# Moving the Q, K and V evictions from ScalarE to VectorE, and the attention scale from the Q eviction into the exponential

## The chip, the cores and the metric

The program runs on the eight cores of one Trainium2 chip. Every core executes the same program on its own two of the 16 sequences; nothing is exchanged between cores. The time of an execution is that of the slowest core, in microseconds (us).

## The reference

For x of shape (16, 2048, 1024), with one attention head of width 128 and a feed-forward part of width 4096:

```
xn  = layernorm(x)
Q, K, V = xn @ Wq, xn @ Wk, xn @ Wv
att = softmax(causal(Q @ K.T * 128**-0.5)) @ V @ Wo
h   = xn @ W1 + b1
h   = h + (cos(th)*wr + sin(th)*wi) * wi * sin(th + 0.1*h) * 0.1
out = x + att + relu(h) @ W2 + b2
```

## The kernel before

A core works through five stages, divided by barriers: stage 1 and attention for its first sequence, the same for its second, then one feed-forward stage over both. Each engine counts up the semaphore sbar at the end of a stage, and each waits for all of them before the next.

**Stage 1** (shown below) takes 16 tiles of 128 tokens. For each tile j:

- SP loads x into one of five buffers (L220). It waits with load j until ScalarE has centred tile j-5.
- VectorE computes mean and variance (two bn_stats, L313 and L314, and bn_aggr, L316).
- ScalarE takes the square root (L362) and writes the centred tile in bf16 (L367), one iteration behind VectorE.
- VectorE inverts the root (L323) and scales the identity matrix by it: diag_li (L328). It does this for tile j-2 after it has done the statistics of tile j. For the first sequence it also does some small operations on prep, a table of 32 columns, three per iteration up to j = 8.
- TensorE transposes the tile by eight products with diag_li (L440) into psTx. ScalarE copies psTx to xn_rg (L380), POOL stores that to the scratch tensor xn_scr (L236), which the feed-forward stage reads back.
- TensorE forms the tile's share of Q, K and V: 24 products, L412, L419 and L426, called qkv_slice(j) in the code. In TensorE's order it stands behind the transposes of tile j+1.

Four tiles make a group: psQ, psK and psVB are one bank each and hold 512 tokens. Only one copy of each exists, so between groups they have to be evicted to Q_fm, K_fm and V_tm. ScalarE does it (L385, L387, L388) right after the copy of the next group's first psTx, and this copy itself waits until the group's products are done, because xn_rg has room for four tiles. qkv_slice of the next group's first tile waits for the three evictions (semaphore sqke). The Q eviction multiplies by QSCALE. The fourth group's evictions stand behind the loop (L392 to L395).

For the first sequence ScalarE also computes an arctangent at j = 14 (L358), which needs another activation table before and after.

After its last store POOL issues the weight loads, W1 in the first sequence (L243) and W2 in the second (L250): four loads each, which convert f32 to bf16 and run while the attention stage runs. The attention blocks are opened with `nc.Block()` and not with no_gpsimd_drain, so that POOL ends them with a drain.

**Attention** takes 16 tiles of 128 queries, each with all keys up to the diagonal: products to psLogA and psLogB, a mask added by a product, exp on ScalarE with row sums (L641, L648, L657), the sums' inverse put on a diagonal by VectorE, transposes (L546), VectorE's evictions of them (L622), the products with V (L560) and ScalarE's copy to o_fm (L665).

**The feed-forward stage** runs 16 groups of 256 tokens through 32 slices of the hidden width; the output accumulates in psOut. It is the same in both kernels.

Of the kernel before, what the change touches and what calls it, by code (L numbers as in the profile page):

```python
# [11 lines left out]
AF = mybir.ActivationFunctionType  # L12
# [13 lines left out]
R1 = 512  # L26
NR1 = T // R1
R3 = 256
NR3 = T // R3
QSCALE = float(DK) ** -0.5  # L30
# [16 lines left out]
def build_nc():  # L47
# [23 lines left out]
    with ExitStack() as ctx:  # L71
# [20 lines left out]
        fc_sb = sbuf("fc_sb", [128, 8], F32)  # L92
# [5 lines left out]
        Q_fm = sbuf("Q_fm", [128, T], BF16)  # L98
# [30 lines left out]
        sqk = sem("sqk")  # L129
# [49 lines left out]
        try:  # L179
          for s in range(NSEQ):  # L180
# [3 lines left out]
            with ExitStack() as pctx:  # L184
# [120 lines left out]
                @blk.vector  # L305
                def _(v):
                    if bar_in:
                        v.wait_ge(sbar.h, bar_in)
                    for j in range(NT1 + 2):
                        if j < NT1:  # L310
                            p2 = 16 * (j % 4)
                            v.wait_ge(sxp[j % 5].h, sxp_b[j % 5] + 16 * (j // 5 + 1))
                            v.bn_stats(stats[:, p2 + 0:p2 + 6], x_sb[j % 5][:, 0:512])  # L313
                            v.bn_stats(stats[:, p2 + 6:p2 + 12], x_sb[j % 5][:, 512:1024])  # L314
                            v.drain()
                            ins = v.bn_aggr(stats[:, p2 + 12:p2 + 14],  # L316
                                            stats[:, p2 + 0:p2 + 12])
                            svar.inc(ins)
                        jj = j - 2
                        if jj >= 0:  # L320
                            p2 = 16 * (jj % 4)
                            v.wait_ge(srst.h, srst_b + jj + 1)
                            v.reciprocal(stats[:, p2 + 14:p2 + 15],  # L323
                                         stats[:, p2 + 15:p2 + 16])
                            if jj >= 2:
                                v.wait_ge(stx.h, stx_b + jj - 1)
                            v.drain()
                            ins = v.tensor_scalar(  # L328
                                diag_li[jj % 2][:], idn_sb[:],
                                stats[:, p2 + 14:p2 + 15], -1.0,  # L330
                                ALU.mult, ALU.mult)
                            sdg3.inc(ins)
                        if j < NT1:
                            for fn in pv.get(j, []):
                                fn(v)
                    v.drain()
                    v.sem_inc(sbar.h, 1)

                @blk.scalar
                def _(sc):  # L340
                    if bar_in:
                        sc.wait_ge(sbar.h, bar_in)
                    sc.wait_ge(sc0.h, 128)
                    if s == 0:
                        sc.activation(col(5), th_sb[:], AF.Sin, scale=1.0 / 16)
                        sc.activation(col(4), th_sb[:], AF.Sin, scale=1.0 / 32)
                        sc.drain()
                        sp1.inc(sc.activation(col(6), col(4), AF.Square), 2)
                    for j in range(NT1 + 2):
                        jj = j - 1  # L350
                        if s == 0 and j == 12:
                            sc.wait_ge(sp2.h, 1)
                            sc.drain()
                            sp3.inc(sc.sign(col(7), col(1)))
                        if s == 0 and j == 14:
                            sc.wait_ge(sp2.h, 2)
                            sc.drain()
                            sp3.inc(sc.activation(col(6), col(5), AF.Arctan))  # L358
                        if 0 <= jj < NT1:
                            p2 = 16 * (jj % 4)  # L360
                            sc.wait_ge(svar.h, svar_b + jj + 1)
                            srst.inc(sc.activation(stats[:, p2 + 15:p2 + 16],  # L362
                                                   stats[:, p2 + 13:p2 + 14],
                                                   AF.Sqrt, bias=fc_sb[:, 0:1]))
                            if jj >= 3:
                                sc.wait_ge(stx.h, stx_b + jj - 2)
                            ins = sc.activation(xn_tm[jj % 3], x_sb[jj % 5][:],  # L367
                                                AF.Identity, scale=-1.0,
                                                bias=stats[:, p2 + 12:p2 + 13])
                            sln.inc(ins)  # L370
                        je = j - 2
                        if 0 <= je < NT1:
                            r, tt = je // 4, je % 4
                            if tt == 0 and r > 0:
                                sc.wait_ge(sqk.h, sqk_b + 4 * r)
                            if je >= 4:
                                sc.wait_ge(sxnst[je % 4].h,
                                           sxnst_b[je % 4] + 16 * (je // 4))
                            sc.wait_ge(stx.h, stx_b + je + 1)
                            stxe.inc(sc.copy(xn_rg[:, tt * 1024:(tt + 1) * 1024],  # L380
                                             psTxB[je % 2][:]))
                            if tt == 0 and r >= 1:
                                rp = r - 1
                                sc.wait_ge(sqk.h, sqk_b + 4 * (rp + 1))
                                sqke.inc(sc.activation(Q_fm[:, rp * R1:(rp + 1) * R1],  # L385
                                                       psQ[:], AF.Copy, scale=QSCALE))
                                sqke.inc(sc.copy(K_fm[:, rp * R1:(rp + 1) * R1], psK[:]))  # L387
                                sqke.inc(sc.copy(V_tm[:, rp * R1:(rp + 1) * R1], psVB[:]))  # L388

                    rp = NR1 - 1  # L390
                    sc.wait_ge(sqk.h, sqk_b + 4 * (rp + 1))
                    sqke.inc(sc.activation(Q_fm[:, rp * R1:(rp + 1) * R1],  # L392
                                           psQ[:], AF.Copy, scale=QSCALE))
                    sqke.inc(sc.copy(K_fm[:, rp * R1:(rp + 1) * R1], psK[:]))
                    sqke.inc(sc.copy(V_tm[:, rp * R1:(rp + 1) * R1], psVB[:]))  # L395
                    sc.drain()
                    sc.sem_inc(sbar.h, 1)

# [57 lines left out]
            with ExitStack() as pctx:  # L456
# [172 lines left out]
                def _(sc):  # L629
                    sc.wait_ge(sbar.h, bar_in)  # L630
                    for qq in range(NT1 + 1):
                        j = qq - 1
                        if qq < NT1:
                            qi = qq
                            if qi >= 2:
                                sc.wait_ge(stx2.h, stx2_b + cum_sg[qi - 1])
                            sc.drain()
                            if qi >= 8:
                                sc.wait_ge(slgA.h, slgA_b + qi - 7)
                                a0 = 16 + 4 * (qi % 2)  # L640
                                ins = sc.activation(p2buf[qi % 2][:, 0:1024],  # L641
                                                    psLogA[:], AF.Exp,
                                                    bias=fc_sb[:, 1:2],
                                                    accum_out=stats[:, a0:a0 + 1])
                                se1.inc(ins)
                                sc.wait_ge(slg.h, slg_b + qi + 1)
                                sc.drain()
                                ins = sc.activation(  # L648
                                    p2buf[qi % 2][:, 1024:(qi + 1) * 128],
                                    psLogB[:, 0:(qi - 7) * 128], AF.Exp,  # L650
                                    bias=fc_sb[:, 1:2],
                                    accum_out=stats[:, a0 + 1:a0 + 2])
                                se1B.inc(ins)
                            else:
                                sc.wait_ge(slg.h, slg_b + qi + 1)
                                a0 = 16 + 4 * (qi % 2)
                                ins = sc.activation(p2buf[qi % 2][:, 0:(qi + 1) * 128],  # L657
                                                    psLogA[:, 0:(qi + 1) * 128],
                                                    AF.Exp, bias=fc_sb[:, 1:2],
                                                    accum_out=stats[:, a0:a0 + 1])  # L660
                                se1.inc(ins)
                        j2 = qq - 1
# [255 lines left out]
```

## Time and profile before

| | us |
|---|---|
| median of 3 runs | 1223.08 (1222.55 to 1224.01) |
| profiled execution, its time | 1225.54 |
| profiled execution, span of the slowest core (core 2) | 1223.8 |
| spans of the eight cores | 1209.9 to 1223.8 |
| core 2: stage 1, first sequence, until 78.7 | 78.7 |
| core 2: attention, first sequence, until 142.3 | 63.6 |
| core 2: stage 1, second sequence, until 194.3 | 52.0 |
| core 2: attention, second sequence, until the feed-forward stage's first product at 264.0 | 69.7 |
| core 2: feed-forward stage | 959.8 |

From 147.0 to 194.3 us, the second sequence's stage 1, ScalarE is busy for 39.3 of 47.3 us, TensorE for 35.8 and VectorE for 24.6. Of the whole span TensorE is busy for 89%.

A row of the timeline gives the start, the duration of one instruction or of a run of alike ones (x8), engine, line, operation, what is written and read, and in brackets how long the engine had been idle and what ended that. PEclk is the clock granted to TensorE as a share of 2.4 GHz.

### The profile page before, as it was taken

To read this page: it belongs to the slowest core of one execution; us is meant where nothing else is said; L and a number is where in the kernel's file an instruction comes from. 1 tells how busy PE (TensorE), PEld (TensorE's weight loads), DVE (VectorE), ACT (ScalarE), POOL (GpSimd) and SP (SyncE) were. 2 spreads that over 40 slices of the span, in tenths; PEclk is the share of its full clock that TensorE was granted. 3 is DMA by queue.
4 is the path that set the end of the run, shared out by engine and by line. 5 is a ranking of instruction groups with operands and counts; after the bars stand their busy time and mean duration, and the time that the engine had idled before them with its cause. 6 is when DMAs were issued, how large, how long until landed. Compare 5 with 4: busy or idle time off the path is not lost.

```text
span 1223.8 us, 23872 instructions; the slowest of 8 cores (1209.9 to 1223.8 us)
## 1 busy us (share of the span) xinstructions
PE 1085.5 (89%) x7936; PEld 736.5 (60%) x7936; DVE 453.2 (37%) x1007; ACT 596.0 (49%) x1285; POOL 37.0 (3%) x48
## 2 busy tenths in 40 slices
PE   0757676759999999999999999999999999999998
PEld 0745475546665666566656665666665666566665
DVE  2725662533333333333333333333333333333333
ACT  2865495525444545444545444545444544444444
POOL 1220031000000000000000000000000000000000
PEclk9976696789999999999999999999999999999999
DMA  7869687940202020202020202020202020202000
GB/s 159 245 118 195 143 251 126 168 119 1 87 1 87 1 87 1 87 1 86 2 87 2 87 1 87 2 86 2 87 1 87 1 87 1 87 1 87 22 32 36
DMA packets 47416, 87.13 MB, mean 71 GB/s; under 512 B 7106, under 2 KB 23490, under 8 KB 46274
## 3 DMA queue, kind: packets, MB, share of 16 engines
q1 hardware_dynamic: 36226, 59.39, 15.2%
q0 software_dynamic: 11072, 26.22, 11.9%
q8 instruction: 68, 1.11, 0.4%
q14 instruction: 50, 0.41, 0.1%
HBM read 78.25 MB, written 25.17 MB: 85 GB/s over the span
## 4 chain that ended last, share of the span: by engine, by line
PE 73%; DVEq 2%; DVE 2%; issue 1%; ACT 1%; ACTq 0%
PE psOut L847 37%; PE psW L821 36%; DVEq L767 2%; DVE probs L769 1%; ACT rb_sb L794 1%; DVE u_sb L746 1%; DVE out_sb L769 0%; PE psOut L837 0%; DVEq L774 0%; DVEq L745 0%; DVEq L766 0%; DVEq L743 0%; ACTq L793 0%; ACTq L791 0%; ACT ss_sb L786 0%
## 5 line engine op out<-in xcount | busy, mean ns | idle before, releaser
L821 PE MATMUL psW<-xn_r,W_sb 128*128 128x256 bf16 x4096 | 538.7, 275 | 8.5 <-PEq L456 8.5
L847 PE MATMUL psOut<-W_sb,rb_sb 128*128 128x512 bf16 x2048 | 531.6, 382 | 10.3 <-ACT rb_sb L794 10.3
L821 PEld LDWEIGHTS psW<-xn_r,W_sb 128*128 128x128 bf16 x4096 | 404.7, 99 | 169.2 <-issue 12.7
L746 DVE SCALAR_TENSOR_TENSOR u_sb<-ss_sb,Rp_sb,psW 128x256 f32<-128x256 bf16 x512 | 244.2, 480 | 592.0 <-ACT ss_sb L786 579.1
L786 ACT ACTIVATE ss_sb<-psW,phb_sb 128x256 bf16<-128x256 f32 x512 | 242.5, 474 | 444.1 <-PE psW L821 444.1
L847 PEld LDWEIGHTS psOut<-W_sb,rb_sb 128*128 128x128 bf16 x2048 | 200.6, 98 | 150.5 <-issue 19.2
L794 ACT ACTIVATE rb_sb<-u_sb,b_sb 128x256 bf16<-128x256 f32 x511 | 254.5, 498 | 57.1 <-DVE u_sb L746 55.1
L622 DVE CAST pT_big<-psT 128x512 bf16<-128x512 f32 (+2 forms) x80 | 48.9, 612 | 42.7 <-PE psT L546 38.5
L440 PE MATMUL psTx<-diag_li,probs 128*128 128x128 bf16 x176 | 15.9, 243 | 40.0 <-DVE diag_li L328 37.0
L546 PE MATMUL psT<-diag_li,xn_rg 128*128 128x128 bf16 x272 | 31.8, 263 | 17.8 <-DVE pT_big L622 15.6
L560 PE MATMUL psO<-pT_big,V_tm 128*128 128x128 bf16 x272 | 31.4, 259 | 17.0 <-DVE pT_big L622 16.3
L769 DVE TENSOR_TENSOR out_sb<-psOut,out_sb 128x512 f32<-128x512 f32 x32 | 20.6, 686 | 51.0 <-PE psOut L847 51.0
L380 ACT CAST xn_rg<-psTx 128x1024 bf16<-128x1024 f32 x32 | 32.4, 1014 | 12.5 <-PE psTx L440 7.6
L440 PEld LDWEIGHTS psTx<-diag_li,probs 128*128 128x128 bf16 x176 | 12.5, 109 | 41.5 <-issue 41.4
L546 PEld LDWEIGHTS psT<-diag_li,xn_rg 128*128 128x128 bf16 x272 | 22.4, 119 | 23.8 <-issue 23.7
L560 PEld LDWEIGHTS psO<-pT_big,V_tm 128*128 128x128 bf16 x272 | 20.2, 111 | 27.0 <-issue 25.4
L837 PE MATMUL psOut<-Wo_sb,o_fm 128*128 128x512 bf16 x64 | 23.6, 376 | 14.6 <-DVE probs L769 9.4
L665 ACT CAST o_fm<-psO 128x128 bf16<-128x128 f32 x32 | 8.5, 266 | 51.9 <-PE psO L560 51.9
L412 PE MATMUL psQ<-xn_rg,Wq_sb 128*128 128x128 bf16 x256 | 22.2, 236 | 11.2 <-ACT V_tm L388 10.9
L236 POOL DMA_DIRECT2D xn_scr<-xn_rg x32 | 27.1, 848 | 156.6 <-ACT xn_rg L380 156.6
L412 PEld LDWEIGHTS psQ<-xn_rg,Wq_sb 128*128 128x128 bf16 x256 | 17.6, 107 | 13.1 <-issue 12.8
L837 PEld LDWEIGHTS psOut<-Wo_sb,o_fm 128*128 128x128 bf16 x64 | 6.1, 96 | 31.2 <-issue 30.9
(91 smaller groups left out, 439.7 us busy)
## 6 DMA issues: line engine op xcount, KB each, us to landing
x_sb<-x SPq DMA_DIRECT2D x52, 512.0 KB, 5.6
W_sb<-w POOLq DMA_DIRECT2D x8, 2048.0 KB, 47.8
xn_scr<-xn_rg POOLq DMA_DIRECT2D x32, 256.0 KB, 4.3
xn_r<-xn_scr SPq DMA_DIRECT2D x16, 512.0 KB, 6.9
out<-out_sb SPq DMA_DIRECT2D x32, 256.0 KB, 2.1
out<-probs SPq DMA_DIRECT2D x32, 256.0 KB, 5.0
xn_r<-x SPq DMA_DIRECT2D x12, 512.0 KB, 6.3
Q_fm<-b2rep SPq DMA_DIRECT2D x1, 512.0 KB, 3.4
```

Of the source, the lines that this page charges most:

```text
L380: stxe.inc(sc.copy(xn_rg[:, tt * 1024:(tt + 1) * 1024], psTxB[je % 2][:]))
L412: t.matmul(psQ[:, tt * 128:(tt + 1) * 128], Wq_sb[:, ci * DK:(ci + 1) * DK], xn_rg[:, tt * 1024 + ci * 128: tt * 1024 + (ci + 1) * 128], s ...
L546: ins = t.matmul(psT2[b][:, (c % 4) * 128:(c % 4 + 1) * 128], p2buf[j % 2][:, c * 128:(c + 1) * 128], diag_li[j % 2][:], start=True, stop= ...
L560: ins = t.matmul(psO[j % 2][:], V_tm[:, c * DK:(c + 1) * DK], pT_big[c // 8][:, (c % 8) * 128:(c % 8 + 1) * 128], start=(c == 0), stop=(c ...
L622: (st2e if b == 0 else st2eV).inc(v.tensor_copy(pT_big[si // 2][:, (si % 2) * 512:(si % 2) * 512 + w], psT2[b][:, 0:w]))
L746: su2.inc(v.scalar_tensor_tensor(u2_sb[ci % 2][:], ss_sb[ci % 2][:], Rp_sb[:, c:c + 1], psW1[slot][:], ALU.mult, ALU.add))
L769: soadd.inc(v.tensor_tensor(out_sb2[j % 2][:, hh * 512:(hh + 1) * 512], psOut[tt][:, hh * 512:(hh + 1) * 512], out_sb2[j % 2][:, hh * 512: ...
L786: ssc3.inc(sc.activation(ss_sb[ci % 2][:], psW1[slot][:], AF.Sin, scale=0.1, bias=phb_sb[:, c:c + 1]))
L794: srb.inc(sc.activation(rb_sb[cp % 3][:], u2_sb[cp % 2][:], AF.Relu, bias=b1_sb[:, (cp % NCF):(cp % NCF) + 1]))
L821: ins = t.matmul(psW1[slot][:], W1_sb[:, k * DFF + c * 128: k * DFF + (c + 1) * 128], xn_r3[g % 2][:, k * R3:(k + 1) * R3], start=(k == 0) ...
L837: t.matmul(psOut[tt][:, h * 512:(h + 1) * 512], o_fm2[gg // NR3][:, c0:c0 + 128], Wo_sb[:, h * 512:(h + 1) * 512], start=True, stop=False, ...
L847: ins = t.matmul(psOut[tt][:, h * 512:(h + 1) * 512], rb_sb[cw % 3][:, tt * 128:(tt + 1) * 128], W2_sb[:, cc * D + h * 512: cc * D + (h + ...
```

## The change

VectorE does the evictions of Q, K and V. Those of group rp stand in its loop at j = 6, 10 and 14, behind the statistics of tile j, the diagonal of tile j-2 and the prep operations of that iteration, ahead of the statistics of tile j+1; those of the last group stand behind the loop. In front of each three it waits for the group's last product and drains. ScalarE's evictions are gone; its wait for the group's products, ahead of the next group's first copy to xn_rg, stays. Q is evicted without its factor, and the three exponentials get scale=QSCALE in its place.

```diff
@@ VectorE, stage 1, in the loop over j
+                        if j >= 6 and (j - 6) % 4 == 0:
+                            rp = (j - 6) // 4
+                            v.wait_ge(sqk.h, sqk_b + 4 * (rp + 1))
+                            v.drain()
+                            sqke.inc(v.tensor_copy(
+                                Q_fm[:, rp * R1:(rp + 1) * R1], psQ[:]))
+                            sqke.inc(v.tensor_copy(
+                                K_fm[:, rp * R1:(rp + 1) * R1], psK[:]))
+                            sqke.inc(v.tensor_copy(
+                                V_tm[:, rp * R1:(rp + 1) * R1], psVB[:]))
+                    rp = NR1 - 1
...
@@ ScalarE, stage 1, behind the copy to xn_rg
-                            if tt == 0 and r >= 1:
-                                rp = r - 1
-                                sc.wait_ge(sqk.h, sqk_b + 4 * (rp + 1))
-                                sqke.inc(sc.activation(Q_fm[:, rp * R1:(rp + 1) * R1],
-                                                       psQ[:], AF.Copy, scale=QSCALE))
-                                sqke.inc(sc.copy(K_fm[:, rp * R1:(rp + 1) * R1], psK[:]))
-                                sqke.inc(sc.copy(V_tm[:, rp * R1:(rp + 1) * R1], psVB[:]))
-
-                    rp = NR1 - 1
...
@@ ScalarE, attention, three times
                                                     psLogA[:], AF.Exp,
+                                                    scale=QSCALE,
                                                     bias=fc_sb[:, 1:2],
```

## Rows read from the trace of the kernel before

**Rows 1.** Stretches: engines' busy time, granted clock, DMA share, GB/s.
```profile
160.00:165.00 5.00, 4.15 (x68) 3.66 (x65) 4.27 (x12) 5.00 (x9) 1.50 (x2) 1.00 0.94 305
...
180.00:185.00 5.00, 2.52 (x32) 2.37 (x29) 0.42 (x2) 4.51 (x8) 0.84 (x1) 0.82 0.44 105
185.00:190.00 5.00, 5.00 (x77) 4.95 (x76) 0.42 (x2) 3.35 (x5) 1.69 (x2) 0.84 0.28 67
...
255.00:260.00 5.00, 0.38 (x4) 0.24 (x4) 0.00 (x0) 0.27 (x1) 0.00 (x0) 0.83 0.16 30
```

**Rows 2.** Timeline, core 2, around the second attention stage.
```profile
191.36 3.60 POOL L250 DMA_DIRECT2D W_sb<-w  x4
...
255.59 0.27 ACT L665 CAST o_fm<-psO 128x128 bf16<-128x128 f32 x1 [4.51 <-PE psO L560]
...
264.04 4.21 PE L821 MATMUL psW<-xn_r,W_sb 128*128 128x256 bf16 x19 [8.54 <-PEq L456]
```

**Rows 3.** Timeline, core 2, second sequence, from first to second group.
```profile
157.40 0.69 DVE L313 BATCH_NORM_STATS2 stats<-x_sb 128x6 f32<-128x512 f32 x1 [2.32 <-DMA x_sb<-x]
157.45 0.61 PE L426 MATMUL psVB<-Wv_sb,xn_rg 128*128 128x128 bf16 x8
...
158.01 0.68 DVE L314 BATCH_NORM_STATS2 stats<-x_sb 128x6 f32<-128x512 f32 x1
158.26 1.01 ACT L380 CAST xn_rg<-psTx 128x1024 bf16<-128x1024 f32 x1 [0.65 <-PE psVB L426]
...
159.11 0.25 DVE L328 TENSOR_SCALAR diag_li<-idn_sb,stats 128x128 bf16<-128x128 bf16 x1
159.17 0.60 ACT L385 ACTIVATE Q_fm<-psQ 128x512 bf16<-128x512 f32 x1
159.27 0.69 DVE L313 BATCH_NORM_STATS2 stats<-xn_r 128x6 f32<-128x512 f32 x1
...
159.61 0.61 PE L440 MATMUL psTx<-diag_li,pT_big 128*128 128x128 bf16 x8 [1.55 <-DVE diag_li L328]
...
160.99 0.61 PE L412 MATMUL psQ<-xn_rg,Wq_sb 128*128 128x128 bf16 x8 [0.77 <-ACT V_tm L388]
...
161.84 1.03 ACT L380 CAST xn_rg<-psTx 128x1024 bf16<-128x1024 f32 x1
```

**Rows 4.** Timeline, core 2, last products of further groups, both sequences.
```profile
39.73 0.61 PE L426 MATMUL psVB<-Wv_sb,xn_rg 128*128 128x128 bf16 x8
...
51.14 0.61 PE L426 MATMUL psVB<-Wv_sb,xn_rg 128*128 128x128 bf16 x8
...
62.16 0.61 PE L426 MATMUL psVB<-Wv_sb,xn_rg 128*128 128x128 bf16 x8
...
168.26 0.61 PE L426 MATMUL psVB<-Wv_sb,xn_rg 128*128 128x128 bf16 x8
...
179.68 0.61 PE L426 MATMUL psVB<-Wv_sb,xn_rg 128*128 128x128 bf16 x8
```

**Rows 5.** Timeline, core 2: the pace of VectorE and of ScalarE.
```profile
33.50 0.69 DVE L313 BATCH_NORM_STATS2 stats<-x_sb 128x6 f32<-128x512 f32 x1
...
36.19 0.69 DVE L313 BATCH_NORM_STATS2 stats<-x_sb 128x6 f32<-128x512 f32 x1
...
163.97 1.03 ACT L380 CAST xn_rg<-psTx 128x1024 bf16<-128x1024 f32 x1
```

**Rows 6.** Groups by shape, until 280 us: VectorE's casts of 512 columns.
```profile
L622 DVE CAST pT_big<-psT 128x512 bf16<-128x512 f32 x56 | 38.7, 692 | 36.6 <-PE psT L546 33.9 <-issue 0.2
```

**Rows 7.** Timeline, core 2: TensorE's first product behind two evictions.
```profile
54.77 0.61 PE L412 MATMUL psQ<-xn_rg,Wq_sb 128*128 128x128 bf16 x8 [2.50 <-ACT V_tm L388]
...
183.22 1.01 PE L412 MATMUL psQ<-xn_rg,Wq_sb 128*128 128x128 bf16 x8 [2.48 <-ACT V_tm L388]
```

**Rows 8.** Timeline, core 2: ScalarE around the first sequence's last group.
```profile
65.26 0.99 ACT L380 CAST xn_rg<-psTx 128x1024 bf16<-128x1024 f32 x1
...
68.83 1.02 ACT L380 CAST xn_rg<-psTx 128x1024 bf16<-128x1024 f32 x1
```

More of the change, by code:

```diff
@@ L335, in _ @@
                                 fn(v)
+                        if j >= 6 and (j - 6) % 4 == 0:
[9 more added lines that the diff above has]
+                    rp = NR1 - 1
+                    v.wait_ge(sqk.h, sqk_b + 4 * (rp + 1))
+                    v.drain()
+                    sqke.inc(v.tensor_copy(
+                        Q_fm[:, rp * R1:(rp + 1) * R1], psQ[:]))
+                    sqke.inc(v.tensor_copy(
+                        K_fm[:, rp * R1:(rp + 1) * R1], psK[:]))
+                    sqke.inc(v.tensor_copy(
+                        V_tm[:, rp * R1:(rp + 1) * R1], psVB[:]))
                     v.drain()
@@ L381, in _ @@
                                              psTxB[je % 2][:]))
-                            if tt == 0 and r >= 1:
-                                rp = r - 1
-                                sc.wait_ge(sqk.h, sqk_b + 4 * (rp + 1))
-                                sqke.inc(sc.activation(Q_fm[:, rp * R1:(rp + 1) * R1],
-                                                       psQ[:], AF.Copy, scale=QSCALE))
-                                sqke.inc(sc.copy(K_fm[:, rp * R1:(rp + 1) * R1], psK[:]))
-                                sqke.inc(sc.copy(V_tm[:, rp * R1:(rp + 1) * R1], psVB[:]))
-                    rp = NR1 - 1
[L391 to L395, printed above, removed]
                     sc.drain()
@@ L650, in _ @@
                                     psLogB[:, 0:(qi - 7) * 128], AF.Exp,
+                                    scale=QSCALE,
                                     bias=fc_sb[:, 1:2],
@@ L658, in _ @@
                                                     psLogA[:, 0:(qi + 1) * 128],
-                                                    AF.Exp, bias=fc_sb[:, 1:2],
+                                                    AF.Exp, scale=QSCALE,
+                                                    bias=fc_sb[:, 1:2],
                                                     accum_out=stats[:, a0:a0 + 1])
```

## The prediction

> **What bounds the kernel now.** I read the spans of all cores first, then the page's slices, then the busy time by stage, then the timeline of stage 1 and of the way into the feed-forward stage. The feed-forward stage holds 959.8 us of core 2's span of 1223.8 and is not touched, so the change can only move its start, 264.04 us [rows 2]. What sets that start is not the second attention stage's arithmetic: ScalarE's last copy of it ends at 255.86, the next product comes at 264.04, and in between only DMA runs, at a share of 0.16 [rows 1, 2]. That is the tail of the W2 loads, which POOL issued at 191.36, behind the last store of stage 1, and which its drain waits for. So on this core the end follows stage 1's last copies; whatever delays them by a microsecond delays W2 and the end by one.
>
> In stage 1 one place matters: the passage from one group of four tiles to the next. Let T be the end of a group's last product, 157.45 + 0.61 = 158.06 in the second sequence [rows 3]. ScalarE copies the next tile at T+0.20, then evicts Q, K and V. The diagonal of the tile after (number 5) leaves VectorE at 159.11, TensorE transposes at T+1.55, then waits until 160.99 for the evictions. ScalarE's copy of this tile starts at 161.84, T+3.78, and the following copy 2.13 later (163.97) [rows 3, 5]. Inside the group ScalarE sets the pace with 2.13 per tile; VectorE needs 159.27 - 157.40 = 1.87 per tile [rows 3]. The intervals from T to T are 11.41 and 11.02 in the first sequence, 10.81 and 11.42 in the second [rows 3, 4].
>
> **The change, part by part.**
>
> ScalarE loses three evictions at each passage. They held it from 159.17, and TensorE resumed on the third at 160.99 [rows 3]. That is about 1.4 us of ScalarE time, worth something only if the diagonal of tile 5 is there early. It is not any more, as the next part shows.
>
> VectorE gets the wait and the three copies ahead of the statistics of tile 7, and the diagonal of tile 5 stands behind these statistics. So what is queued behind the waiting VectorE is: two bn_stats and a bn_aggr (for which ScalarE's root of tile 7 waits, and behind it SP's load of tile 12), and the diagonal of tile 5, for which TensorE waits, and after it ScalarE and POOL's store. A cast of 512 columns out of PSUM takes 0.69 [rows 6]; two VectorE instructions in a row start 158.01 - 157.40 = 0.61 apart [rows 3]. I take release and drain as the 0.20 that ScalarE needs now [rows 3], so the third cast lets go at T + 0.20 + 3 x 0.61 + about 0.1 = T+2.1 (T+2.3 if none overlap). From the first bn_stats to the diagonal are 159.11 - 157.40 = 1.71, from there to TensorE's transposes 0.50, and 0.7 on to ScalarE's copy (0.61 and a release of 0.1) [rows 3]. So the transposes of tile 5 start at T + 2.1 + 1.71 + 0.50 = T+4.3 and its copy at T+5.0, where it is T+3.78 now: **1.2 us later at a passage**. TensorE is idle for some 4 us there. Everything cheap that used to cover the diagonal has gone: it was made while the products of the old group still ran.
>
> Then the rest of the group. ScalarE: copy 7 starts at 5.0 + 2 x 2.13 = T+9.3, ends at 10.3, and the last products take 0.1 + 1.5 (three runs of eight, 0.45 apart, the last of 0.61): T+12.0. VectorE: from T+2.1 three tiles of 1.87 and then 1.71 to the diagonal of tile 8, 0.5 to TensorE, 0.45 to the products and 1.5 for them: T+11.9. Both give an interval of 12.0. Against the measured ones [rows 3, 4]:
> - second sequence, first and second interval: 12.0 - 10.81 = +1.2 and 12.0 - 11.42 = +0.6;
> - first sequence, second interval: 12.0 - 11.02 = +1.0;
> - first sequence, first interval: VectorE has the prep operations too and takes 36.19 - 33.50 = 2.69 per tile [rows 5] for tiles 7 and 8, some 2.1 for tile 9. Tile 8's diagonal is then at 2.1 + 2 x 2.69 + 2.1 + 1.71 = T+11.3, the last product ends at T+13.7: 13.7 - 11.41 = +2.3.
>
> The last group. In the second sequence its end hangs on TensorE: three times transposes and products of one tile at 1.78 (four runs of eight, 0.45 apart), then 1.5, from T+4.3: T+11.1 at full clock. Now the last evictions wait for a product that ends 11.03 after T (ScalarE's idle time ends at 191.41): +0.1. In the first sequence ScalarE is late at this passage because of the arctangent and its tables: T is 62.77, and its copy 12 starts only at 65.26, copy 13 at 68.83 [rows 4, 8]. With the evictions gone copy 13 can follow copy 12 by 2.13, once VectorE's diagonal has come: T+5.0 = 67.8. This is 1.0 earlier, of which TensorE's tail keeps about 0.4: -0.4.
>
> The evictions behind the loop are on VectorE 2.1 us from T, on ScalarE 0.1 + about 1.7: +0.3, counted once, for the first sequence alone. In the second the W2 loads end later than attention by far more than this [rows 2].
>
> The exponentials get a factor. The nearest row is the Q eviction, which carries the same factor and takes 0.60 [rows 3]; 48 exponentials cost nothing by it, and 0.5 us if each costs 0.01. I take 0.
>
> Sum without the clock: 2.3 + 1.0 - 0.4 + 0.3 + 1.2 + 0.6 + 0.1 = +5.1.
>
> **The clock.** TensorE now sits idle for some 4 us at each of the six passages. Today's idle stretches there are at most 2.5 us long, and their outcome differs: behind 2.48 us the products run at 1.2 GHz (eight in 1.01), behind 2.50 at 2.4 GHz (eight in 0.61) [rows 7]. One such slow stretch shows as 0.82 and 0.84 of the clock in two slices of 5 us: (0.18 + 0.16) x 5 / 0.5 = 3.4 us at half speed, 1.7 us of lost work [rows 1]. Where TensorE has slack little of that reaches the end; my chains have about 0.5 to 0.9 of slack in the middle groups, so up to 1.2 reaches T there (three intervals, 3.6), 1.7 in the second sequence's last group, and almost nothing in the first interval, which waits for VectorE. If all fell: +5.3. I take half, +2.7. The Trainium skill's page "TensorE: Matmul & The Clock Gate", section "HAM oscillation — how this bites in real kernels", says that a stream of matmuls broken by long idle gaps falls back to the lower clock at every gap; by it the sum would be +10.4 and not +7.8. The rows above show both outcomes behind gaps of 2.5 us, and none of 4 us inside stage 1.
>
> **Sum:** +7.8, on the profiled execution 1225.5 to 1233.3. It stands 2.5 above the median, so the median goes to **1231**.
>
> **The rivals.**
> - *The clock falls at every passage, and costs more in the group than I allow.* +5.1 + 5.3 = +10.4, with VectorE's casts at no overlap (6 x 0.2) +11.6, and to +15 if the delays add up behind each other in the chains: 1235 to 1238. For it: the longer idle time. Against: one of the two present ones of 2.5 us did not trip it.
> - *DMA hides it.* From 160 to 165 us the DMA share is 0.94 at 305 GB/s, and VectorE waits 2.32 us for the x of tile 7 at 157.40 [rows 1, 3]. A group moves four loads of 512 KB and four stores of 256 KB, 3.1 MB, about 10.3 us at this rate. If stage 1 ran by DMA, VectorE would only wait for Q, K, V where it waits for x today, and nothing would be lost: 0 to +2, 1223 to 1225. Against: my interval of 12.0 is longer than 10.3, and the wait for x at 157.40 ended before ScalarE needed that diagonal.
> - *ScalarE's relief wins.* If ScalarE is the late one at a passage, taking 1.43 us off it brings the copy of tile 5 forward. This happens where its copy 4 starts later than T+1.4, as at the first sequence's arctangent (T+2.5). At all six passages it would be -8.6: 1214.5. For it: ScalarE is the busiest engine of stage 1 and sets the pace inside a group. Against: elsewhere copy 4 starts at T+0.20 [rows 3], long before that point.
> - *The W2 tail changes its length.* The 7.6 us between attention's end and the feed-forward stage are a DMA tail at a share of 0.16 [rows 1, 2]. Moved against other traffic it could be shorter or longer by some 2 us; it widens the range in both directions.
>
> **How the numbers follow.** My forecast (+4 to +10) has 0.62, the dearer clock 0.16, DMA cover 0.13, ScalarE's relief 0.09. 0.2% is 2.4 us, about what a measurement of this kernel tells from no change. Slower 0.78, same 0.13, faster 0.09. The range reaches from 1225 (upper end of the DMA case) to 1238 (upper end of the clock case).
>
> **What would show it.** VectorE has 24 more casts of 512 columns from psQ, psK and psVB, of 0.69 each. TensorE's idle time before L440 ends on VectorE's diagonal at six passages, after about 4 us, and its wait for the evictions is gone. The intervals from T to T are about 12 to 13.5 us. ScalarE's idle time before its copies to xn_rg grows. The granted clock in stage 1 is lower. POOL issues W2 some 5 to 10 us later than 191.36; the feed-forward stage is as long as before. I am wrong if VectorE's copies end well before T+2, if the intervals stay under 11.5, or if the feed-forward stage starts at a time that does not follow W2's issue.

## The result, and the profile after

| | before | changed |
|---|---|---|
| median of 8 runs each, us | 1224.21 | 1236.55 |
| ratio | | 1.0102 (1.009 to 1.0114) |
| profiled execution, its time | 1225.54 | 1235.43 |
| its span, slowest core | 1223.8 | 1233.5 |

The kernel became slower by 1.02%, 12.5 us (11.0 to 14.0); forecast were +7.8. Each median includes one execution of over 1300 us, which the ratio leaves out.

T is again the end of a group's last product. The passage from the second to the third group of the second sequence, changed kernel, core 2, from the timeline:

```profile
172.91 0.61 PE L431 MATMUL psVB<-Wv_sb,xn_rg 128*128 128x128 bf16 x8
173.68 0.69 DVE L340 CAST Q_fm<-psQ 128x512 bf16<-128x512 f32 x1 [3.71 <-PE psVB L431]
173.72 1.01 ACT L399 CAST xn_rg<-psTx 128x1024 bf16<-128x1024 f32 x1 [0.99 <-PE psVB L431]
174.28 0.68 DVE L342 CAST K_fm<-psK 128x512 bf16<-128x512 f32 x1
...
174.88 0.68 DVE L344 CAST V_tm<-psVB 128x512 bf16<-128x512 f32 x1
...
175.48 0.68 DVE L313 BATCH_NORM_STATS2 stats<-x_sb 128x6 f32<-128x512 f32 x1
...
177.17 0.25 DVE L328 TENSOR_SCALAR diag_li<-idn_sb,stats 128x128 bf16<-128x128 bf16 x1
...
177.68 1.01 PE L445 MATMUL psTx<-diag_li,probs 128*128 128x128 bf16 x8 [4.16 <-DVE diag_li L328]
...
178.78 1.01 ACT L399 CAST xn_rg<-psTx 128x1024 bf16<-128x1024 f32 x1 [2.82 <-PE psTx L445]
...
180.19 1.06 PE L431 MATMUL psVB<-Wv_sb,xn_rg 128*128 128x128 bf16 x8
...
182.74 0.61 PE L424 MATMUL psK<-xn_rg,Wk_sb 128*128 128x128 bf16 x8
...
186.76 0.61 PE L431 MATMUL psVB<-Wv_sb,xn_rg 128*128 128x128 bf16 x8
```

Beside [rows 3]: T is 173.52. VectorE sits idle for 3.71 us until 173.68, casts Q, K and V, and only then does the statistics; the diagonal comes at T+3.65, TensorE transposes at T+4.16 (it was T+1.55), ScalarE's second copy starts at T+5.26 (it was T+3.78). ScalarE, relieved of 1.43 us, spends 2.82 us idle in their place. From 177.68 to 182.7 eight products take 1.01 to 1.06 us, at 182.74 again 0.61: TensorE's clock. The third group ends at 187.37, an interval of 13.85.

The stretches of the changed kernel, core 2 (engines' busy time, granted clock, DMA share, GB/s), 5 us from the end of the idle time, and the second stage 1 as a whole:

```profile
177.50:182.50 5.00, 4.83 (x46) 4.86 (x47) 4.63 (x13) 2.55 (x4) 0.85 (x1) 0.50 0.57 163
149.20:203.90 54.70, 38.24 (x513) 37.38 (x514) 30.75 (x81) 33.58 (x45) 16.59 (x20) 0.78 0.65 184
```

and the same stage of the kernel before:

```profile
147.30:194.50 47.20, 35.80 (x513) 33.96 (x514) 24.34 (x69) 38.98 (x57) 16.63 (x20) 0.86 0.72 214
```

The granted clock is 0.50, 1.2 GHz, over a stretch in which TensorE is busy for 4.83 of 5.00 us, right behind 4.16 us of idle time. Over the stage it falls from 0.86 to 0.78. The passage one group earlier on the same core had the same idle time and another outcome at first:

```profile
164.58 0.61 PE L445 MATMUL psTx<-diag_li,pT_big 128*128 128x128 bf16 x8 [4.16 <-DVE diag_li L328]
...
166.16 1.06 PE L431 MATMUL psVB<-Wv_sb,xn_rg 128*128 128x128 bf16 x8
...
169.33 0.61 PE L431 MATMUL psVB<-Wv_sb,xn_rg 128*128 128x128 bf16 x8
```

Here the products start at 0.61 and become slow about 1.1 us later, until about 169.1, some 3.4 us of slow time; this interval is 13.09. Each of this core's six passages has such a stretch. So have those of the other seven cores: in the timelines of one profiled execution each, all 48 passages of the changed kernel show TensorE idle for 4.16 us and behind it a stretch of at least 2.5 us in which eight products take over 0.85 us. In the kernel before 24 of 48 show one, though TensorE's single waits there are shorter. Between the first and the last T of each sequence such slow time adds up to 25.2 us per core in the changed kernel and to 11.5 in the kernel before.

TensorE's waits from 20 to 205 us, core 2, changed kernel (in total, times, longest; the longest is the program's start), and then before:

```profile
PE psTx L445 <- DVE diag_li L328: 59.4, 13, 24.9
```

```profile
PE psTx L440 <- DVE diag_li L328: 39.6, 8, 27.1
PE psQ L412 <- ACT V_tm L388: 10.9, 6, 2.5
```

The wait for the evictions has gone and that for the diagonal has grown by more: without the start 34.5 us, before 12.5 + 10.9 = 23.4.

The evictions themselves, as groups by shape, and the exit of the second stage 1, changed kernel, core 2:

```profile
L340 DVE CAST Q_fm<-psQ 128x512 bf16<-128x512 f32 x6 | 4.1, 691 | 17.0 <-PE psVB L431 17.0
L344 DVE CAST V_tm<-psVB 128x512 bf16<-128x512 f32 x6 | 4.1, 679 | 0.0
```

```profile
200.13 0.61 PE L431 MATMUL psVB<-Wv_sb,xn_rg 128*128 128x128 bf16 x8
200.78 3.60 POOL L250 DMA_DIRECT2D W_sb<-w  x4
...
202.11 0.68 DVE L353 CAST V_tm<-psVB 128x512 bf16<-128x512 f32 x1
203.74 2.17 SPq L583 DMA_DIRECT2D xn_r<-xn_scr  x2
```

A cast takes 0.68 to 0.69, as [rows 6]. POOL issues W2 at 200.78, 9.4 later than in [rows 2].

To compare the kernels I took the ends of the groups' last products from the timelines of all eight cores of one profiled execution each. A "first" interval runs from the first group's T to the second's, and so on. The mean intervals, in us; "sum" is that of the six, and "measured" is (ratio - 1) x 1224:

| kernel | first sequence | second sequence | sum | against before | measured |
|---|---|---|---|---|---|
| before | 11.2, 11.2, 13.6 | 10.7, 11.0, 10.5 | 68.1 | | |
| changed | 13.8, 13.2, 12.9 | 13.4, 13.8, 13.4 | 80.4 | +12.2 | +12.5 |
| e1_fill | 13.8, 12.4, 11.1 | 11.8, 11.8, 11.1 | 71.9 | +3.8 | +3.8 |
| e2_later | 12.6, 10.5, 13.2 | 10.4, 11.0, 8.9 | 66.5 | -1.6 | -0.7 |
| e4_wait | 12.7, 11.4, 13.8 | 11.4, 11.0, 10.9 | 71.2 | +3.1 | +2.2 |
| e7_best | 12.5, 10.5, 12.0 | 10.7, 10.8, 8.8 | 65.3 | -2.9 | -2.1 |
| e8_fill_before | 10.7, 11.3, 12.4 | 10.7, 10.9, 9.9 | 66.0 | -2.1 | -2.1 |

The six intervals account for the whole difference within about 1 us in every row. That is also their own scatter: e3_scale, which does the same work in stage 1 as the kernel before, has a sum of 69.1 against 68.1. The delay is made in stage 1 and passes through everything behind it.

### The profile page after: what moved, and what is told of

It reads as the page before. It is cut to its first block, busy times and chain, and to the rows that moved or that the text cites. A ratio compares the mean times of both kernels' runs of the same rounds, so it can differ in the third digit from the quotient of the medians.

```text
span 1233.5 us, 23880 instructions; the slowest of 8 cores (1227.8 to 1233.5 us)
## 1 busy us (share of the span) xinstructions
PE 1089.8 (88%) x7936; PEld 741.8 (60%) x7936; DVE 466.9 (38%) x1031; ACT 584.7 (47%) x1261; POOL 37.0 (3%) x48
## 4 chain that ended last, share of the span: by engine, by line
PE 72%; DVEq 2%; DVE 2%; issue 1%; ACT 1%; ACTq 0%
PE psOut L855 36%; PE psW L829 36%; DVEq L775 2%; DVE probs L777 1%; ACT rb_sb L802 1%; DVE u_sb L754 0%; DVE out_sb L777 0%; PE psOut L845 0%; DVEq L782 0%; DVEq L753 0%; DVEq L774 0%; DVEq L751 0%; ACTq L801 0%; ACTq L799 0%; ACT ss_sb L794 0%
## 5 line engine op out<-in xcount | busy, mean ns | idle before, releaser
L445 PEld LDWEIGHTS psTx<-diag_li,probs 128*128 128x128 bf16 x176 | 13.6, 115 | 56.9 <-issue 56.9
L424 PE MATMUL psK<-xn_rg,Wk_sb 128*128 128x128 bf16 x256 | 23.2, 243 | 0.0
```

The source lines that it names most:

```text
L445: ins = t.matmul(psTxB[j % 2][:, c * 128:(c + 1) * 128], xn_tm[j % 3][:, c * 128:(c + 1) * 128], diag_li[j % 2][:], start=True, stop=True, ...
```

## The experiments

**e1_fill: keep TensorE's clock.** The changed kernel plus:

```diff
                         if j >= 1:
                             qkv_slice(j - 1)
+                        if j in (4, 8, 12):
+                            for _ in range(16):
+                                t.matmul(psD[:], idn_sb[:], Wq_sb[:, 0:512],
+                                         start=True, stop=True,
+                                         skip_group_check=True)
```

> The changed kernel, with 16 extra products of 512 columns that TensorE writes to the free eighth PSUM bank behind the last product of the first three groups of each sequence (96 in all; their result is not read). They fill about 3.5 us of the 4.2 us in which TensorE waits for VectorE's diagonal. Theory (order of VectorE's work costs 1.2 us at a passage, and the clock that falls in the idle time costs 1 to 2 us more): the granted clock in both stages 1 goes back to 0.95 or more, the intervals between group ends fall from 13.1 to 13.9 to about 12.0 (12.7 to 13.8 stay in the first sequence's first interval, which waits for VectorE), and the time falls by 6 to 9 us against the changed kernel, to 1227 to 1231. Rival (the intervals are long because of VectorE's own work or of DMA, the clock only fell along with it): intervals and time stay within 2 us of the changed kernel, 1235 to 1238.

Measured: 1226.65 us, ratio 1.0031 (1.0018 to 1.0043). Core 2, timeline, and the two stages 1:

```profile
172.37 0.61 PE L432 MATMUL psVB<-Wv_sb,xn_rg 128*128 128x128 bf16 x8
173.03 3.40 PE L456 MATMUL psD<-Wq_sb,idn_sb 128*128 128x512 bf16 x15
...
176.63 0.26 DVE L329 TENSOR_SCALAR diag_li<-idn_sb,stats 128x128 bf16<-128x128 bf16 x1
...
177.14 0.61 PE L446 MATMUL psTx<-diag_li,probs 128*128 128x128 bf16 x8 [0.70 <-DVE diag_li L329]
...
177.83 1.01 ACT L400 CAST xn_rg<-psTx 128x1024 bf16<-128x1024 f32 x1 [2.41 <-PE psTx L446]
...
184.14 0.61 PE L432 MATMUL psVB<-Wv_sb,xn_rg 128*128 128x128 bf16 x8
```

```profile
27.00:81.00 54.00, 43.08 (x559) 35.40 (x562) 36.56 (x108) 36.08 (x48) 16.40 (x20) 1.00 0.70 186
149.80:199.00 49.20, 42.94 (x558) 35.82 (x562) 30.58 (x81) 33.12 (x45) 16.59 (x20) 0.93 0.76 205
```

The diagonal is exactly as late as in the changed kernel (T+3.65, transposes at T+4.16 from T = 172.98), but the products behind it take 0.61, and the interval is 11.78 in place of 13.85. The granted clock of the second stage 1 is 0.93, under the 0.95 expected; the missing part lies in its first group, ahead of any passage, and from the first T on it is 1.00. Slow time between the sequences' first and last T is 0.2 us per core, where it was 25.2. Work whose result nobody reads, put into idle time, makes the changed kernel 0.7% faster. So of the 12.5 us, 8.7 are the lower clock behind the late diagonal, and 3.8 are left. The 3.8 are not the late diagonal alone, because the kernel before loses some time to its clock as well: e8_fill_before, below, makes it 5.9 with the clock kept in both.

**e2_later: the same casts one iteration later.**

```diff
-                        if j >= 6 and (j - 6) % 4 == 0:
-                            rp = (j - 6) // 4
+                        if j in (7, 11, 15):
+                            rp = (j - 7) // 4
```

> The changed kernel with VectorE's evictions in the loop one iteration later, at j = 7, 11 and 15, so that the diagonal of the next group's second tile is made before VectorE waits. Theory (the place in VectorE's order is what costs): TensorE transposes that tile at about T+1.5 as in the kernel before, the copy follows at T+2.4 instead of T+3.8, intervals of 9.7 to 10.9 us, where DMA (3.1 MB a group) begins to set the pace; clock as before; the time is 0 to 6 us below the kernel before, 1218 to 1224. Rival (VectorE is too busy for these casts wherever they stand): intervals of 12 us or more and over 1230.

Measured: 1222.81 us, ratio 0.9994 (0.9984 to 1.0004). Core 2, timeline, and one stretch:

```profile
157.13 0.61 PE L431 MATMUL psVB<-Wv_sb,xn_rg 128*128 128x128 bf16 x8
157.13 0.25 DVE L328 TENSOR_SCALAR diag_li<-idn_sb,stats 128x128 bf16<-128x128 bf16 x1
157.63 0.61 PE L445 MATMUL psTx<-diag_li,pT_big 128*128 128x128 bf16 x8
...
159.10 0.68 DVE L344 CAST V_tm<-psVB 128x512 bf16<-128x512 f32 x1
...
160.04 0.61 PE L417 MATMUL psQ<-xn_rg,Wq_sb 128*128 128x128 bf16 x8 [1.79 <-DVE V_tm L344]
160.09 1.00 ACT L399 CAST xn_rg<-psTx 128x1024 bf16<-128x1024 f32 x1
```

```profile
165.00:170.00 5.00, 3.64 (x60) 3.17 (x57) 4.03 (x12) 3.53 (x6) 0.84 (x1) 1.00 1.04 321
```

The diagonal leaves VectorE while the old group's last products still run; ScalarE's second copy starts at 160.09, T+2.35 from T = 157.74, where it was T+3.78 in [rows 3]. So ScalarE's relief is worth its 1.43 us here. VectorE has as many casts as in the changed kernel: the place in its order, with the clock that falls behind it, cost 13 us (1.0102 against 0.9994), not the work. The time is that of the kernel before, but not every interval is: the first sequence's first, in which VectorE also has the prep operations, is 1.4 us longer, and the second sequence's last is 1.6 shorter (8.9 against 10.5). The first two intervals of the second sequence hardly fall below those of before. The DMA share is 1.04 there, and VectorE waits 5.4 us in that stage for x on core 2 (before 5.8, with the changed kernel 0.6); I read this as DMA setting the pace, but no run made the loads lighter. At the passage of the first sequence's last group all eight cores still have a slow stretch.

**e3_scale: the factor alone.** The evictions stay on ScalarE, Q as a plain copy, `scale=QSCALE` in the three exponentials.

> The kernel before, evictions on ScalarE, with only the factor moved: Q is evicted by a plain copy and the three exponentials get scale=QSCALE. Theory: no change, within 1 us of the kernel before. Rival (a factor in an exponential costs 10 ns or more each): 0.5 to 1 us slower, with the ACTIVATE rows of the exponentials longer by that.

Measured: 1224.1 us, ratio 0.9998 (0.9979 to 1.0018). A group by shape of e3_scale, core 2; before, the same instructions (L648) took 1114 on the mean:

```profile
L647 ACT ACTIVATE xn_rg<-psLogB,fc_sb 128x1024 bf16<-128x1024 f32 x2 | 2.2, 1113 | 0.2
```

The 16 exponentials of full width from psLogA take 1113 with the factor and 1114 without. The rows show no cost of the factor; the time alone, with an interval of 0.2% to either side, could not have told 0.5 us from nothing.

**e4_wait: the wait without the casts.** The kernel before plus, at the same place in VectorE's loop:

```diff
+                        if j >= 6 and (j - 6) % 4 == 0:
+                            rp = (j - 6) // 4
+                            v.wait_ge(sqk.h, sqk_b + 4 * (rp + 1))
+                            v.drain()
```

> The kernel before with only VectorE's wait for the group's last product and its drain, at j = 6, 10 and 14; the evictions stay on ScalarE. Theory (the casts ahead of the statistics are what makes the diagonal late, the wait by itself is covered by ScalarE's evictions): the diagonal of the next group's second tile leaves VectorE at about T+2.0, TensorE transposes at T+2.5, ScalarE's copy stays at about T+3.8; time within 2 us of before. Rival (the wait alone costs): intervals 1 us longer or more and 5 us or more in all.

Measured: 1225.5 us, ratio 1.0018 (1.0008 to 1.0029): slower by 2.2 us, a little beyond what the theory expected. Core 0, timeline:

```profile
160.13 0.61 PE L430 MATMUL psVB<-Wv_sb,xn_rg 128*128 128x128 bf16 x8
...
162.67 0.69 DVE L328 TENSOR_SCALAR diag_li<-idn_sb,stats 128x128 bf16<-128x128 bf16 x1
...
163.61 0.61 PE L444 MATMUL psTx<-diag_li,pT_big 128*128 128x128 bf16 x8 [2.87 <-DVE diag_li L328]
...
164.52 1.03 ACT L384 CAST xn_rg<-psTx 128x1024 bf16<-128x1024 f32 x1
...
166.76 0.69 DVE L313 BATCH_NORM_STATS2 stats<-xn_r 128x6 f32<-128x512 f32 x1 [1.98 <-DMA xn_r<-x]
```

From T = 160.74 ScalarE's second copy starts at T+3.78, to the hundredth as before: at the passage the wait is covered. What it costs shows in the first intervals of both sequences (+1.4 and +0.7 in the table). In the first sequence VectorE has the prep operations to do; the two cores whose clock holds there (1 and 5) take 13.0. In the second sequence it is mostly the clock again, because one wait of 2.87 us has taken the place of 1.55 and 0.77:

```profile
176.44 1.01 PE L444 MATMUL psTx<-diag_li,probs 128*128 128x128 bf16 x8 [2.87 <-DVE diag_li L328]
```

This is the same core one passage later, and here the products behind 2.87 us run at half speed. Of the second sequence's first intervals those of cores 1, 3, 6 and 7 have a stretch like this and take 11.3 to 11.7 us; those of cores 2, 4 and 5 have none of this length and take 10.7 to 10.8, as before. Core 0 takes 12.8: it comes to wait for x (1.98 us) a tile further on; whether VectorE's wait caused that was not tried. Of all 48 passages of e4_wait 30 have a slow stretch.

**e5_w2_before and e6_w2_after: without the last W2 load,** before and changed, `range(4)` to `range(3)` and the counts of swr lowered by 16. These two kernels leave out the fourth quarter of W2: the feed-forward stage reads the third in its place (`cc % 24`), with as many products as before and a wrong output.

> The kernel before without the last of the four W2 loads (4 MB of 16 MB read less; the feed-forward stage takes the third quarter of W2 twice in its place, with as many products as before). Theory (the tail of the W2 loads sets the feed-forward stage's start on the slow cores): the gap from ScalarE's last copy of the second attention stage to the first feed-forward product, 1.1 to 8.2 us on the eight cores, is 1 to 2 us on all of them, and the slowest core ends 4 to 8 us earlier, 1215 to 1220. Rival (the gap is the drain itself and does not hang on the loads): gap and time stay, 1223 to 1225.

> The changed kernel with the same cut in the W2 loads. Theory (the delay of stage 1 goes through to the end whichever of the two, arithmetic or W2, ends last): the distance to the kernel before with the same cut stays 10 to 14 us, so 1226 to 1233. Rival (the W2 tail swallowed part of the delay, or made part of it): the distance is under 8 us or over 16 us.

Measured: 1217.69 us, 0.9953 (0.9935 to 0.9971), and 1230.64 us, 1.0058 (1.0042 to 1.0073). The feed-forward stage's first products with the idle time before them, e5_w2_before, core 7:

```profile
L821 PE MATMUL psW<-xn_r,W_sb x152: 272/273/421, 256.9 to 289.7; 128*128 128x256 bf16 x152
its engine sat idle before it (us, times) until:
  issue: 1.7, 1
  PEq L456: 1.5, 1
```

The gap from ScalarE's last attention copy to the first product is 1.1 to 1.2 us on all eight cores of both kernels; it was 1.1 to 8.2 before ([rows 2]) and 1.1 to 8.6 with the change. So the tail of the W2 loads is what the late cores wait for, and it costs the kernel 5.8 us (3.5 to 8.0). The quotient of the two ratios is 1.0058 / 0.9953 = 1.0105, that of the two kernels with all of W2 1.0102: the tail neither swallows nor makes a part of the delay.

**e8_fill_before: the clock in the kernel before.** Six products of 512 columns where TensorE waits for the evictions, ahead of `qkv_slice(j - 1)` at j = 5, 9 and 13.

> The kernel before with 6 extra products of 512 columns (1.3 us) between the transposes of a group's second tile and the products of its first, where TensorE waits for ScalarE's evictions (at j = 5, 9, 13). Theory (with idle time of at most 2.5 us the clock falls only at some passages, and there it costs 0.4 to 0.7 us each): clock in both stages 1 at 0.97 or more, time 0 to 3 us below the kernel before. Rival (a low clock costs the kernel before as much as the changed one, so it explains no part of the difference): 6 us faster or more.

Measured: 1221.25 us, ratio 0.9983 (0.9971 to 0.9994), 2.1 us faster. The granted clock of core 2's two stages 1 is 0.96 and 0.94, less than the 0.97 expected, but slow time between the sequences' first and last T falls from 11.5 to 1.3 us per core, and one passage of 48 keeps a stretch. The lower clock costs the kernel before about a quarter of what it costs the changed one. With the clock kept in both, the two kernels are 1.0031 / 0.9983 = 1.0048 apart, 5.9 us.

**e7_best: e2_later with both ideas.** Seven such products at j = 4, 8 and 12, and K of the last group on ScalarE:

```diff
+                    sc.wait_ge(sqk.h, sqk_b + 4 * NR1)
+                    sqke.inc(sc.copy(K_fm[:, (NR1 - 1) * R1:NR1 * R1], psK[:]))
                     sc.drain()
```

> The version with VectorE's evictions one iteration later, with two additions: 7 extra products of 512 columns in TensorE's idle time behind the first three groups, and in the last group K evicted by ScalarE beside Q and V on VectorE. Theory (DMA now sets the pace inside the second sequence's stage 1, the clock costs little): 0 to 3 us faster than without the additions, so 1219 to 1223, mostly from the first sequence. Rival (the clock still costs in that version): 5 us faster or more.

Measured: 1221.64 us, ratio 0.9983 (0.997 to 0.9995). It beats the kernel before by 2.1 us, no more than the filling alone does in e8_fill_before. Against e2_later the gain is in the first sequence (its intervals add up to 35.0, there 36.2), none in the second (30.2, there 30.3).

**e9_w2_late: e7_best, and the feed-forward stage no longer waits for all of W2.**

```diff
-                            swr.inc(g.dma_start(dstw, srcw), 16)
+                            (swl if jw == 3 else swr).inc(
+                                g.dma_start(dstw, srcw), 16)
...
-                blk = pctx.enter_context(nc.Block())
+                blk = pctx.enter_context(nc.Block(no_gpsimd_drain=(s == 1)))
...
                             t.wait_ge(srb.h, srb_b + cw + 1)
+                            if cw == 24:
+                                t.wait_ge(swl.h, 16)
```

> The version with VectorE's evictions one iteration later, the extra products and K on ScalarE behind the loop, and with the feed-forward stage no longer waiting for all of W2: the fourth load has a semaphore of its own, for which TensorE waits at the 25th slice of the first group, some 40 us into that stage, and the second attention stage ends without POOL's drain. Theory (on the slow cores the tail of the W2 loads sets the feed-forward stage's start): the gap from ScalarE's last copy to the first feed-forward product is 1 to 3 us on all cores where it was 1.1 to 10.1, and the time is 3 to 7 us below the same version without this, 1214 to 1219. Rival (the first three loads end as late as the fourth, because they share the DMA engines): gap and time as without it, 1221 to 1223.

Measured: 1216.64 us, ratio 0.9938 (0.9915 to 0.9961), the fastest version. The gap is 1.1 to 1.2 us on all cores, where it was 1.1 to 10.1 in e7_best. About 5.5 of its 7.6 us come from the wait that the prediction met on its way to the end (0.9938 against e7_best's 0.9983), and the other 2.1 are e7_best's. The semaphore of its own and the missing drain were not tried apart.

## Why the prediction was right, and where its sizes were off

The direction, the place and the mechanism were right: VectorE's diagonal comes late, TensorE's idle time and the chain behind it grow, and the clock falls. The size was not: 12.5 us lie outside the band of +4 to +10 to which I gave 0.62, and inside that of the rival with the dearer clock.

- *The passage, 1.2 us.* Right: transposes at T+4.16 for a forecast T+4.3; the copy at T+4.85 with the clock kept (177.83 in e1_fill), T+5.26 without, for T+5.0. e2_later shows that it is the order: the same casts behind the diagonal cost nothing on balance.
- *The intervals, 12.0 and 13.7 in the first.* With the clock kept they are 11.8, 12.4 and 13.8. For the second sequence's last group I had 11.1, and e1_fill has 11.1.
- *The sum without the clock, +5.1.* Measured +3.8 (2.2 to 5.3). The largest difference is the first sequence's last interval, -2.5 where I had -0.4. The 13.6 of before contain a stretch at 1.2 GHz on all eight cores, which I had left in my figure for after; e8_fill_before puts about 1.1 on it (12.4). The remaining 1.3 (12.4 to 11.1) I read as ScalarE's relief at the arctangent, of which I had let only 0.4 arrive: on core 2 its copy 13 starts at T+4.9 in e1_fill and at T+5.6 in e8_fill_before. Against e8_fill_before, where both keep their clock, the intervals differ by 71.9 - 66.0 = 5.9.
- *The exit, +0.3.* Not there. From the first stage 1's last T to attention's first product are 3.2 us on the mean before and 3.2 after. VectorE's casts end later than ScalarE's did, but in the second stage 1 the next stage starts 203.74 - 202.79 = 0.95 us behind the last one, where behind ScalarE's it took 1.37 (192.97 to 194.34).
- *The exponentials, 0.* Right, by the rows of e3_scale.
- *The clock, +2.7.* This is the term that was mis-sized: it is 12.5 - 3.8 = 8.7 us. It went wrong in two steps. First, I took half of the passages, and all 48 have a stretch. Half was the share of the kernel before (24 of 48), whose waits are shorter; I carried it over to waits of 4.16 us. I also wrote that the present waits are at most 2.5 us long, and core 2 has one of 2.95, with a slow stretch two microseconds on:

```profile
65.71 0.61 PE L440 MATMUL psTx<-diag_li,probs 128*128 128x128 bf16 x8 [2.95 <-ACT probs L367]
...
67.97 1.01 PE L412 MATMUL psQ<-xn_rg,Wq_sb 128*128 128x128 bf16 x8 [1.65 <-ACT V_tm L388]
```

  Second, the price if all fell was +5.3, and it is 80.4 - 71.9 = 8.5 by the intervals. The stretch is 3.4 to 5.2 us long on core 2, where I had 3.4 from [rows 1]. By interval, e1_fill against the changed kernel: 0 in the first, which waits for VectorE, as I had it; +0.8, +1.6 and +2.0 where I allowed 1.2 each; +2.3 for 1.7 in the second sequence's last group; and +1.8 in the first sequence's last group, for which I had no clock term at all, without a reason. The rival of a dearer clock was the case that came true; I gave it 1235 to 1238 and 0.16. The rule of the Trainium skill's page "TensorE: Matmul & The Clock Gate", section "HAM oscillation — how this bites in real kernels", that the clock falls at every long gap, agrees with this trace, at 0.50 behind 4.16 us of idle time, and would have been the better choice than one half.
- *DMA hides it.* Not with intervals of over 12 us, as forecast: VectorE's waits for x before L313 in core 2's second stage 1 fall from 5.8 us to 0.6. What keeps e2_later from its gain in the second sequence is probably DMA; that was not shown.
- *W2 sets the end.* Right as a mechanism, by e5_w2_before; and the delay passes through in full, by e6_w2_after.

## What to carry to other kernels

Work moved to an engine with room costs by what stands behind it in that engine's order: three casts and a wait that cost 12.5 us in all became free on balance when they were put behind one diagonal of 0.25 us. Where a change opens an idle gap of some 4 us in TensorE, price the products behind it at half the clock, at every gap, and do not take the share of slow passages from shorter gaps. Look for the longest gap that the trace has, and count over all cores. And read what the last stage waits for before tuning an early one: the tail of a weight load was worth 5.8 us here, more than all that these versions gained at the passages (2.1).

## What the runs showed of the hardware

- Behind 4.16 us without a product TensorE's products fell to 1.2 GHz at all 48 passages of the eight cores, in some only about 1 us after they had begun again at 2.4 GHz. On core 2 the slow stretch was 5.1 to 5.2 us long where it began at once in the second sequence and about 3.5 where it began late, with TensorE busy throughout (4.83 of 5.00 us, granted clock 0.50).
- Shorter waits have both outcomes: behind 2.87 us (e4_wait, core 0) the products ran at 2.4 GHz at 163.61 and at 1.2 GHz at 176.44, and behind 2.5 us the kernel before shows both [rows 7].
- The end of the W2 loads moves little and holds up all engines: on core 2 the DMA share is 0.16 at 30 GB/s from 255 to 260 us [rows 1], and the wait behind ScalarE's last copy is 8.2 us there and 1.1 on cores 4 and 7. Without the fourth load it is 1.1 to 1.2 on all eight.
